# Two items a step, a transposed residual, and scores and values on row tiles of the array

## The reference, cut to what matters

```python
x = x + tanh(g_xattn[0]) * cross_attention(layernorm(x), ctx)     # once, all 16 items
y = layernorm(x)
for i in range(6):
    y = attn_layer(shift_tokens(y), Wqkv[i], qs[i], ks[i], Wo[i]) + y
    y = ffn_layer(shift_tokens(y), g[i], bln[i], W1[i], b1[i], W2[i], b2[i]) + y
x = x + tanh(g_ffn[0]) * y

def attn_layer(x, ...):      # q, k, v = x @ Wqkv, 16 heads of 64 each
    q, k = l2norm(q) * qs, l2norm(k) * ks;  q, k = rotary(q), rotary(k)
    # windows of 32 queries that see their own and the previous window (64 keys), band mask
    return softmax(8 * q k^T + mask) v  @ Wo

def ffn_layer(x, ...):       # xn = layernorm(x) * g + bln;  a, gate = split(xn @ W1 + b1)
    return a * gelu(gate) @ W2 + b2
```

## Time and profile before

| | us |
|---|---|
| median of three runs | 1717.99 (1716.4 to 1719.74) |
| profiled execution, time | 1719.63 |
| profiled execution, span | 1717.8 |
| busy in the span: PE, PEld | 1641.1, 1390.2 |
| busy in the span: ACT, DVE, POOL | 1541.2, 1467.8, 1403.3 |

### The profile page before, as it was taken

One profiled execution on the slowest core, in us unless ns is written; L12 is line 12 of the kernel. 1 busy time (PEld: TensorE's weight loads), 2 busy tenths in 40 slices (PEclk: granted clock), 3 DMA queues, 4 the chain that ended last, 5 costly groups with the idle time before them and its releaser, 6 DMA issues.

```text
span 1717.8 us, 64013 instructions
## 1 busy us (share of the span) xinstructions
PE 1641.1 (96%) x20016; PEld 1390.2 (81%) x20016; DVE 1467.8 (85%) x3219; ACT 1541.2 (90%) x3285; POOL 1403.3 (82%) x1502
## 2 busy tenths in 40 slices
PE   4489999999999999999999999999999999999996
PEld 2368888888888888888888888888888888888885
DVE  4578888888888888888888888888889889888884
ACT  3379999999999999999999999999999999999995
POOL 1388888888888888888888888888888888888882
PEclk8699999999999999999999999999999999999999
DMA  5012322122322222222222322222232212222122
GB/s 140 23 38 66 87 61 70 49 76 54 88 58 66 63 55 75 76 67 55 69 61 58 75 73 70 54 69 57 61 91 57 64 44 64 50 57 57 49 64 59
DMA packets 71323, 110.42 MB, mean 64 GB/s; under 512 B 9716, under 2 KB 36472, under 8 KB 71288
## 3 DMA queue, kind: packets, MB, share of 16 engines
q1 hardware_dynamic: 71288, 110.01, 25.4%
HBM read 20.85 MB, written 1.05 MB: 13 GB/s over the span
## 4 chain that ended last, share of the span: by engine, by line
PE 42%; ACT 18%; issue 17%; DVE 8%; POOL 7%; ACTq 1%; POOLq 1%; DVEq 1%; DMA 1%; SPq 0%
PE bank L1059 7%; PE bank L994 7%; PE bank L987 6%; PE bank L989 5%; PE bank L988 5%; PE bank L1037 5%; POOL u L390 3%; ACT L620 3%; ACT kT L575 3%; POOL P L412 2%; PE bank L1110 2%; PE bank L1071 2%; ACT qbd L567 2%; ACT L623 2%; ACT P L588 2%
## 5 line engine op out<-in xcount | busy, mean ns | idle before, releaser
L390 POOL TENSOR_TENSOR u<-u,t 128x512 f32<-128x512 f32 x384 | 493.6, 1285 | 22.2 <-DVE u L790 21.6
L405 POOL TENSOR_TENSOR u<-u,rn 128x512 f32<-128x512 f32 x384 | 393.1, 1045 | 85.6 <-ACT rn L557 80.0
L987 PE MATMUL bank<-Wl,xsh 128*128 (+1 forms) x576 | 270.2, 469 | 3.5 <-issue 2.0
L790 DVE TENSOR_TENSOR u<-bank,TC 128x512 f32<-128x512 f32 x384 | 260.8, 679 | 3.4 <-ACT sq L538 3.4
L781 DVE TENSOR_REDUCE ss<-sq 128x8 f32<-128x512 f32 x384 | 259.9, 677 | 3.7 <-ACT sq L538 0.7
L1037 PEld LDWEIGHTS bank<-kT,qbd 128*64 128x64 f32 x6144 | 195.2, 138 | 61.2 <-issue 61.2
L538 ACT ACTIVATE sq<-bank 128x512 f32<-128x512 f32 x384 | 230.3, 600 | 15.4 <-PE bank L989 6.0
L567 ACT COPY qbd<-bank 64x512 f32<-64x512 f32 x384 | 222.9, 581 | 11.1 <-PE bank L994 7.7
L989 PE MATMUL bank<-Wh,xsh 128*128 (+1 forms) x576 | 228.9, 397 | 0.0
L988 PE MATMUL bank<-Wh,xsl 128*128 (+1 forms) x576 | 226.9, 394 | 0.0
L994 PE MATMUL bank<-shape_constants,u 128*128 128x128 f32 x1536 | 225.1, 278 | 0.0
(11 more groups left out here) (118 smaller groups left out, 3862.6 us busy)
## 6 DMA issues: line engine op xcount, KB each, us to landing
Pbd<-PT SPq DMA_DIRECT2D x384, 128.0 KB, 2.3
vs<-v SPq DMA_DIRECT2D x96, 384.0 KB, 3.3
Wraw<-in_L_ffn_Wqkv_dram SPq DMA_DIRECT2D x72, 117.5 KB, 2.2
WB<-in_L_ffn_Wo_dram SPq DMA_DIRECT2D x6, 512.0 KB
WB<-in_L_ffn_b_dram SPq DMA_DIRECT2D x6, 341.0 KB
Wraw<-in_L_ffn_W_dram SPq DMA_DIRECT2D x12, 116.0 KB, 2.3
H<-in_x_dram SPq DMA_DIRECT2D x2, 512.0 KB, 5.6
v<-in_ctx_dram SPq DMA_DIRECT2D x2, 512.0 KB, 6.9
```

The source lines that it names most:

```text
L390: nc.gpsimd.tensor_tensor(u[:, slot, c], u[:, slot, c], t2[:, c % 2], ALU.add).then_inc(add_done[c], 1)
L405: nc.gpsimd.tensor_tensor(by_head(u[:, slot, c]), by_head(u[:, slot, c]), spread(rn[:, slot, HC * c:HC * c + HC], HC, DH), ALU.mult).then_ ...
L790: nc.vector.tensor_tensor(by_head(u[:, slot, c]), by_head(bank_of("chunk", c)[:]), TC[:, layer(n), c % 2].broadcast_to([128, HC, DH]), ALU ...
L987: nc.tensor.matmul(out, xh_, Wl[:, w], start=True, stop=False)
```

## The change

- A step handles a pair of items r = 0, 1 (48 pairs); the only lags left are 0 and 1. `n = pair * 2 + r`. One pair is one body of the loop.
- The residual is kept transposed, R[feature, item, token + 1], so the shift of tokens is an offset in the read. `turn_x`, `shift`, `turn_normal`, `turn_h` and POOL's `copy_x` go. The mean is removed by a product with I - 1/128 (`centre`), the variance is taken by a product with 1/128 (`variance`), both 256 columns wide for a pair. `project_out`, `up` and `down` have the weights as stationary operand and 256 moving columns, once for a pair. b1 and b2 become per-partition biases.
- `scores` and `values` are 32 products each half, 64 an item each, on 64 rows of the array: scores 64 rows by 32 columns with 64 (or 32) moving columns, values 64 rows by 64 columns with 32 moving columns. The two row halves write different banks. `qbd` and `Pbd` with their DMAs go; `qT` is filled by one copy of 128 partitions.
- Chunk 3's table product goes to DVE; `raw_copy` goes. Norms of an item: one bound, one logarithm, one exponential for all four chunks. The tables of gelu are loaded once for a pair; value times gate goes from POOL to DVE.
- Wo, W2 and the split W1 have one buffer each; W1 is placed by two DMAs a layer (`place_up`). Before the loop the normal form is transposed into R (8 transposes for every eight items, 4 copies). After it 32 products turn R back, then eight DVE operations and four DMAs finish.

```diff
+        R = sb("R", [128, NB, S + 1])
+        qT = sb("qT", [128, 2, 4, 128])
-        qbd = sb("qbd", [128, 2, 4, 4, 2, WINDOW])
-        Pbd = sb("Pbd", [128, 2, 2, 4, 128])
...
-            def weights_of(n, s):
-                sp.wait_ge(PT_ready[s], n_(n) + 1)
-                sp.wait_ge(pv_full[s], n_(n))
-                for h in range(2):
-                    r = slice(64 * h, 64 * h + 64)
-                    sp.dma_start(Pbd[r, h, s].rearrange("p t n -> p (t n)"), PT[r, s]).then_inc(Pbd_full[s], 16)
+            def place_up(l):
+                sp.wait_ge(W_split, (l + 1) * (NB // 2) + START)
+                if l >= 1:
+                    sp.wait_ge(xf_read, n_(LAYER_PAIRS * l))
+                at = l % 2 * W_SPLIT_SIZE + QKV
+                for dst, src in ((W1h, Wh), (W1l, Wl)):
+                    sp.dma_start(dst[:].bitcast(F32), src[:, at:at + 2 * DI].bitcast(F32)).then_inc(w1_loaded, 16)
...
 POOL, the order of a step
+                if splitting:
+                    split_low()
                 if on(1):
+                    divide(1, 1, 1)
+                    divide(0, 1, 1)
+                if on(0):
+                    add(1, 0, 0)
+                    add(0, 0, 0)
                     bound_norms(0, 0)
+                    add(3, 0, 0)
+                    normalise(1, 0, 0)
+                    add(2, 0, 0)
+                    normalise(0, 0, 0)
+                    normalise(3, 0, 0)
+                    normalise(2, 0, 0)
+                    add(1, 0, 1)
+                    bound_norms(0, 1)
+                    add(0, 0, 1)
+                    add(3, 0, 1)
+                    normalise(1, 0, 1)
+                    normalise(3, 0, 1)
+                    add(2, 0, 1)
+                    normalise(2, 0, 1)
+                    normalise(0, 0, 1)
+                    divide(1, 0, 0)
+                    divide(0, 0, 0)
...
 DVE, the start of a step
+                if on(0):
+                    x_rest(0, 0)
+                if on(1):
+                    maxima(1, 1, 1)
+                    maxima(0, 1, 1)
+                    minus_maxima(1, 1, 1)
+                    minus_maxima(0, 1, 1)
+                    row_sums(1, 1, 1)
+                    row_sums(0, 1, 1)
+                if on(0):
+                    x_rest(0, 1)
+                    squares(1, 0, 0)
+                    squares(0, 0, 0)
+                    swapped(1, 0, 0)
+                    swapped(0, 0, 0)
+                    straight(1, 0, 0)
...
+                def deviations(lag):
+                    pair = it - lag
+                    act.wait_ge(xc_full, n_(pair) + 1)
+                    act.wait_ge(var_full, n_(pair))
+                    nc.scalar.activation(sqx[:], bank_of("xc")[:, 0:2 * S], ACT.Square).then_inc(lsq_done, 1)
...
 PE
+                    for t2_ in range(2):
+                        for h in range(2):
+                            for w2 in range(2):
+                                for a in range(2):
+                                    for e in range(2):
+                                        f = slice(64 * e, 64 * e + 64)
+                                        w, t = 2 * h + w2, 2 * t2_ + a
+                                        seen = slice(max(32 * w - 32, 0), 32 * w + 32)
+                                        at = 256 * s + 128 * t2_ + 64 * h
+                                        i = nc.tensor.matmul(
+                                            bank_of("scores", e, r)[64 * w2 + 32 * a:64 * w2 + 32 * a + 32,
+                                                                    at + (32 if w == 0 else 0):at + 64],
+                                            qT[f, s, t, 32 * w:32 * w + 32], kT[f, s, t, seen], start=False,
+                                            stop=True, skip_group_check=True)
...
+                    for t in range(INNER // 128):
                         for w2 in range(2):
                             for e in range(2):
+                                for h in range(2):
+                                    p, head = slice(64 * h, 64 * h + 64), (2 * t + e) * DH
+                                    at = 128 * (t // 2) + 64 * w2 + 32 * (t % 2)
+                                    i = nc.tensor.matmul(
+                                        bank_of("values", h, r)[64 * e:64 * e + 64, 64 * t + 32 * w2:64 * t + 32 * w2 + 32],
+                                        (vs, v)[w2][p, r, head:head + DH], PT[p, r, e, at:at + 32], start=True, stop=True)
+                    i.then_inc(pv_full, 1)
...
+                    for k in range(INNER // 128):
+                        i = nc.tensor.matmul(bank_of("Wo")[:, 0:2 * S], WoS[:, k], OT[:, k].rearrange("p r s -> p (r s)"),
                                              start=(k == 0), stop=(k == INNER // 128 - 1))
...
 PE, the end of a step
+                    turn_qk(2, 0, 1)
+                    second_values_bank(0, 0)
+                    turn_qk(0, 0, 1)
+                    scores(1, 0, 1)
+                    scores(0, 0, 1)
+                    turn_p(1, 0, 0)
+                    turn_p(0, 0, 0)
```

More of the change, by code:

```diff
@@ L191, in peeled @@
             def peeled(it):
-                step(it, it % 2, lambda lag: 0 <= it - lag < N, SPLIT_LAG + 1 <= it < SPLIT_LAG + N - NB)
-            both = (N - NB + 1 + SPLIT_LAG - LAST) // 2
-            rest = LAST + 2 * both
-            tail = rest + (N - rest) // 2 * 2
-            for it in range(LAST):
-                peeled(it)
-            with eng.Fori(0, both) as pair:
-                for k in range(2):
-                    step(pair * 2 + LAST + k, (LAST + k) % 2, lambda lag: True, True)
@@ L229, in bank_left @@
-        def bank_left(it, kind, k=0):
-            users = next(users for users in BANK_USERS if (kind, k) in users)
-            place = users.index((kind, k))
+                step(it, lambda lag: 0 <= it - lag < PAIRS, SPLIT_LAG <= it < SPLIT_LAG + PAIRS - LAYER_PAIRS)
+            first, rest = LAST + 1, SPLIT_LAG + PAIRS - LAYER_PAIRS
+            for it in range(first):
+                peeled(it)
+            with eng.Fori(0, rest - first) as k:
+                step(k + first, lambda lag: True, True)
@@ new lines, in pipeline @@
+            with eng.Fori(0, PAIRS - rest) as k:
+                step(k + rest, lambda lag: True, False)
+            for it in range(PAIRS, PAIRS + LAST):
+                peeled(it)
+        OF_PAIR = ("Wo", "xc", "up", "down")
+        FREED = {"chunk": lambda k: [sq_done[k], rot_done[k], t2_done[k]],
+                 "v": lambda k: [v_ready[k]],
+                 "turn_qk": lambda k: [k_ready[k // 2] if k % 2 else q_ready[k // 2]],
+                 "scores": lambda k: [sc_out[k]],
+                 "turn_p": lambda k: [PT_ready[k]],
+                 "values": lambda k: [OT_ready[k]],
+                 "Wo": lambda k: [res_done],
+                 "xc": lambda k: [xng_done],
+                 "up": lambda k: [[gelu_done], [hh_ready], [hh_ready]][k],
+                 "down": lambda k: [h_ready]}
@@ L236, in bank_left @@
-                lags, readers = FREED[other]
-                n = it + turns - lags[ok]
-                if not isinstance(it, int) or 0 <= n < N:
-                    return [(r, n_(n + NB if r is h_ready else n) + 1) for r in readers(ok)]
-            return []
-        def weights(n, at, size, rows=128):
-            return WB[0:rows, ds(((n // NB) % 2) * W_SIZE + at, size)]
-        def layer(n):
-            return ds(n // NB, 1)
-        def row_of(t, n):
-            return t[:, ds(n % NB, 1)].rearrange("p o d -> p (o d)")
+                other, ok, orr, lag = users[at]
@@ new lines, in bank_left, with column @@
+                pair = it + turns - lag
+                if not isinstance(it, int) or 0 <= pair < PAIRS:
+                    if other in OF_PAIR:
+                        return [(s, n_(pair + (LAYER_PAIRS if s is h_ready else 0)) + 1) for s in FREED[other](ok)]
+                    return [(s, n_(pair * 2 + orr) + 1) for s in FREED[other](ok)]
+            return []
+        def column(at, pair, per=1, k=0, rows=slice(0, 128)):
+            return fc[rows, ds(pair // LAYER_PAIRS * per + (at + k), 1)]
```

1120 lines of the change are left out of this document (530 added, 590 removed).

## The result

The changed kernel takes 1665.07 us (median of four, 1663.53 to 1665.9) against 1718.45 in the same session: a ratio of 0.969, 95% interval 0.967 to 0.971. It is faster, by 53 us, where 118 were forecast.

A forecast was written before the change was run, and what follows sets the result against it. PE was taken to bound the kernel, at 30.6 us a pair after the change, 31.0 with queue losses. Start 79, first step 27, 47 steps 1457 and tail 38 gave 1601, stated as 1600 us; range 1530 to 1720.

The forecast's parts named there:

- Start: Span before the first step: 73.4 us as before, plus copies and transposes of the items, about 79 us.
- First step: The first pair's step, without lag 1 work beside it: 27 us.
- 47 steps at 31.0: The remaining pair steps at the forecast pace of 31.0 us each: 1457 us.
- the loop: From scores through DVE, POOL, transposes and query copy back to scores: 29.7 us a pair, just under PE's 30.6.
- Tail: From the last scores through softmax, projection, feed-forward, turning products and last DMA: 38 us.
- in-order queues lose a little to each other: Allowance for PE and the loop being so close: 0.4 us added, giving 31.0 us a pair.
- PE's own work: PE's need after the change: 11.7 us other work plus 3.6 small matmuls, 15.3 an item, 30.6 a pair.
- The small matmuls: Scores and values on PE: 256 an item, 3.6 us against 4.3 before; lower bound 3.3, upper bound 8.7.
- my slots of 68 ns: Each array tile holds a small matmul 68 ns: four tiles give 17 ns in values, eight 8.5 in scores.
- Row halves apart: Rival: row halves don't overlap on PE, small matmuls 6.5 us an item, 36.5 a pair, 1870 us; chance 0.12.
- A fixed slot for each pair: Rival: every small load and matmul needs 34 ns whatever its tile, 40.8 us a pair, about 2075; chance 0.05.
- The third rival: The loop through DVE and POOL, not PE, sets the pace: 32.6 us a pair, 1678 us; chance 0.19.

The follow-up runs named there:

- Experiment 3: Changed kernel with the first scores, scores(0,0,0), moved ahead of both up calls on PE: 1642.2 us, ratio 0.954 to the kernel before.
- experiment 2: Changed kernel leaving out four of the eight products of the output projection, 1.73 us of PE work a step: 1619.52 us, one run.
- Experiment 1: Changed kernel with the row-half loops outermost in scores and values, so neighbouring small matmuls share a row half: 1963.27 us, one run.
- experiments 7 to 10: Kernel before with row-tile scores and values alone, one item a step, in four orders: ratios 1.212, 1.226, 1.178 and 1.206.
- experiment 9: Kernel before with row-tile scores and values alone, second half's probabilities turned earlier and ACT's copy of them moved up: 2028.82 us, ratio 1.178.

## Why the prediction was wrong in size

By its own terms, from the table of steps above (1601 forecast, 1664.0 measured):

- **Start**, 79 forecast: 77.7, 1.3 less. **First step**, 27: 30.0, 3 more, at a granted clock of 0.84.
- **47 steps at 31.0**, 1457: 1515.8, that is 58.8 more. The three steps from 107.70 us took 36.7, 36.2 and 33.2 where the steady step takes 32.06: together they cost 13 over the forecast's 31.0 each. In them PE waits once for 2.6 us before scores, 1.7 before values and 1.5 for the lower part of the weights that POOL splits, at clocks of 0.95 to 0.99. I had given the loop no run-in. The other 44 steps (43 of 32.1, one of 30.9) cost the remaining 46.
- **Tail**, 38: 40.5.

**The step that failed** is "in-order queues lose a little to each other: I add 0.4 and take 31.0 us a pair". They lose 1.9. PE's own work was forecast as 30.6 us a pair and is 30.2, so the net error is 1.06 us a step, 46 us over 44 steps, three quarters of the whole miss of 63. The 0.4 had no row behind it. I had compared totals of one step (29.7 for the loop, 30.6 for PE) and not the four places where PE's order reads something only just made. Experiment 3 shows the mechanism for the longest of these waits: covered by 0.75 us of scores, it gives 23 us back. For the other three the cause is read from the trace, and no run took them off at a gain.

The chain that the prediction read as PE alone for whole items is that of the last 199.5 us. In the long stretch ahead of it the other engines stood in the chain as well, so a loop through them must already have been about as long as PE's work; PE was idle for only 7 us there, and its price of an item stands.

The loop of the changed kernel was priced too low as well, at 29.7 us a pair; experiment 2 shows it at 31.1, by a way that also passes through centring and `up`. So even without the four waits this order would have run at some 31.1, not at PE's 30.2, and the forecast's 31.0 lay at the edge of what it can do.

**The order of magnitude of such waits** could have been had from rows: the way residual, centre, square, logarithm, exponential, normal form, two parts passes from one to another of PE, ACT and DVE nine times; with ACT's other copies in between, the last stretch alone, from the end of L979 to `up`, is 4.2 us. In the kernel before, that way was spread over the lags; with a lag of 1 it had to fit between two bursts of one step. The prediction wrote "a spread over five steps becomes one over two", as a point for the rival.

**The terms that were right.** The small matmuls: 3.4 us an item against the 3.6 taken (scores 10.7 ns against 11, values 15.6 against 17), far from the upper bound of 8.7. Experiment 1 shows that alternating row halves, each with its own bank, is what brought values from 28.5 to 15.6. PE is busy for 95.7% of the steady stretch (over 95% forecast), ACT 12.2 us an item (12 to 12.5), POOL 11.9 (12.3), DVE 27.8 a pair ("rather 27").

**The rivals.** Row halves apart would have cost 1870 us; experiment 1, built so, took 1963. Its step at full clock is no dearer than the rival's (35.9 us against 36.5: the bursts cost 5.4 us an item instead of 6.5, and the waits come on top); the lower clock brings the mean to 38.4. A fixed slot for each pair (2075) is excluded by the bursts. The third rival gave nearly the measured time (1678 against 1664) but not by its mechanism: in the changed kernel PE waits for POOL four times only, 5.5 us in all, and POOL waits itself, 195 us ahead of its adds alone, where the changed page shows:

```profile
L378 POOL TENSOR_TENSOR u<-u,t 128x512 f32<-128x512 f32 x384 | 489.3, 1280 | 194.9 <-DVE u L771 108.2
```

And PE, whose work is 30.2 of 32.06 us, answers to what is taken from it (experiment 2), until the loop takes over at 31.1. The rival's mechanism is thus the next limit, less than 1 us away.

**The rule of the Trainium skill** (TensorE: Matmul & The Clock Gate, "Wait — 56ns, not 53.3ns?"), that starts never lie closer than about 25 ns, is contradicted for row and column tiles. PE's instructions inside a burst of values, two rows of eight matmuls each:

```profile
825.98 0.30 PE L1056 MATMUL bank<-PT,vs 64*64 64x32 f32 x8
826.10 0.30 PE L1056 MATMUL bank<-PT,v 64*64 64x32 f32 x8
```

A row starts 0.12 us behind the other, so eight starts take 0.12 us, 15 ns apart on average. The forecast was right not to follow it.

## What to carry to other kernels

When stages spread over many steps are drawn into one or two, price every place where the busiest engine reads what another has just made, one by one along the slower engines' order, and not as a lump: here four such places of 0.3 to 0.75 us took back 1.9 us of a 32 us step. Only the longest was covered at a gain; the three tries at the others each brought a wait elsewhere, so try such moves singly and keep the one that pays. To find how near the next limit is, leave out some work of the busiest engine and read the chain: here it changed from PE to a loop after 1 us. A faster product form can lose several times its gain if it ties the engines to one another's order (1.18 to 1.23 times the time in four orders, for a product 0.9 us an item faster).

## What the runs showed of the hardware that I had not expected

- Alternating row halves (and with them banks) matters much more for values (64 x 64 tiles, 28.5 to 15.6 ns) than for scores (64 x 32 tiles, about 13.4 to 10.7), so the gain doesn't come from a simple count of tiles: by my slots of 68 ns the eight tiles of scores should have reached 8.5 ns, and the four column quarters of one row half 17.
- The granted clock fell in two unlike cases. In experiment 1 PE was busy for 97% of the stretch (1280.49 of 1325 us) and the mean was 0.92, in the one run made. In experiments 7 to 10 PE idled for some 0.7 to 2.5 us at a time in every item (the rows of waits above), and the mean of the whole profiled run was 0.93 to 0.94. What lowers the clock in either case is not shown. The kernels before and after have 1.00 in the steady stretch. Page rows of experiment 1 and then of experiment 9:

```profile
PEclk8799789978999889998899998899989999989997
```

```profile
PEclk8789999989998999899999989999999899999997
```
